# A spectral tower's head stage with the order of a slot changed: a half layer crosses into the next slot

## The chip, the cores and the metric

The kernel runs on one core of one Trainium2 chip. The metric is the device time of one execution in microseconds (us); lower is better. It is written with a queue of instructions for each engine, and the engines wait for each other only by semaphores: TensorE (matrix products and transposes into PSUM banks), ScalarE (activations), VectorE, GpSimd (POOL) and SyncE (SP, which issues the DMAs).

## The reference, cut to what matters

128 images of 64 x 64 with 3 channels go through a tower: a lift to 32 channels with a layer norm, four layers of a spectral convolution plus a pointwise one, and then a head per pixel. The attention and the mixture of experts that follow are not touched by this change.

```
h = layer_norm(x @ fc0_w + fc0_b)
for i in range(4):
    x1 = irfft2(mix of the 2 x 12 x 12 lowest modes of rfft2(h))
    x2 = conv_w[i] h + conv_b[i]
    h = layer_norm(x1 + x2); if i < 3: h = gelu(h)
h = gelu(h @ fc1_w + fc1_b)        # 32 -> 128
h = gelu(h @ fc2_w + fc2_b)        # 128 -> 64
h = h @ fc3_w + fc3_b              # 64 -> 1, one value a pixel
h = h + attention(layer_norm(h)); h = h + ffn(layer_norm(h))
```

## The kernel before

The 128 images are 32 quads of four. Each quad passes the phases stem, layer, layer, layer, head, so that the quads are counted n = 0 to 159, and the quads of the phase "head" are n = 128 to 159. In that phase the fourth layer's output (inverse transform and convolution, then the norm) is made, and the finished pixels of the quad before go through `fc1`, `fc2`, `fc3`. A quad is four slots, k = 0 to 3, and a slot works on one pair of images in two units of half the width, called v and v+1 in the head and `unit`, `unit + 1` in the layer. The head's slots of this kind ("inner") are those of quads 129 to 159, 124 slots, and four closing slots without layer work.

In a slot TensorE runs, in an order written out by hand:

- `inv_h` (L886): the inverse along h into both halves of `ps_y`; `conv` (L893): the convolution, added to one half of `ps_y`, so that ScalarE can read it (`square` L1100, `keep_y` L1104).
- `turn_out` (L905): four transposes of a normalised unit (`normed` L1230 on VectorE) into `ps_t1`; VectorE copies them to `xt` (`take_xt` L1279). These are shown in the trace as `w_raw`, whose room `xt` uses.
- `fc1` (L976 and L983): the first layer for one unit, two products into `ps_f` and two into `ps_s`, each with 32 rows of the array; ScalarE's `g1` (L1123) makes one gelu out of each.
- `fc2` (L992): the second layer for half of a unit, always into the one bank `ps_t2`; ScalarE's `g2` (L1128) empties it. An `fc2` waits for the `g1` of its half and for the `g2` of the half before.
- `fc3` (L1001): the third layer for the whole pair, into `ps_t1`, a slot late; VectorE adds the bias (`take_tok` L1290).
- in slots k = 0 and 2 `inv_w` (L872): the inverse along w of half a quad into `ps_s`, which VectorE transposes (`turn_z` L1211, the name of the memory it writes is `z_second` or `big`). So half of the slots have the inverse and half do not.
- in quads 129 to 135, at the start of slots k = 1 and 3, `mix` (L962): the mixing of modes of the last quads' chunks into `ps_f`, read by VectorE (L1271, L1273) before the next `fc1` may write there.

VectorE also reduces the squares (`sums` L1237) and, each second slot, makes the reciprocal roots of the norm in nine small operations (`rsqrt_half`, L1243 to L1259). Quads 136 to 158 run in a loop of the queues, the others are written out.

Of the kernel before, what the change touches and what calls it, by code (L numbers as in the profile page):

```python
# [7 lines left out]
QUADS = B // 4  # L8
# [18 lines left out]
def vit_tower(nc, x, p, cst, out, scratch):  # L27
# [5 lines left out]
    with ctx:  # L33
# [792 lines left out]
        def _(pe):  # L826
# [35 lines left out]

            def inv_w(n, j, fw_count, g1_count):

                i = n - QUADS
                wait(pe, "y_loaded", 64 * i + 64)
                wait(pe, "iw_read", 2 * i + j)
                wait(pe, "fw_read", fw_count)
                wait(pe, "g1_done", g1_count)
                for sx in range(2):  # L870
                    r = slice(64 * sx, 64 * sx + 64)
                    last = mm(ps_s[:, sx, 0:RUN], c_inw[r, :, :, :].rearrange("p i h w -> p (i h w)"), y_kt[r, j, :],  # L872
                              start=True, stop=True)
                last.then_inc(s["iw_done"], 1)
# [131 lines left out]
            def body(n, q, front, back1, back2, nxt, ph, part=None, chunk=None, seq=None, mixed=0):  # L1006
# [3 lines left out]
                for k in range(4):  # L1010
# [15 lines left out]
                    seen = mixed if part is None or k % 2 == 0 else mixed + (2 if k == 1 else PARTS[part][1] - 2)  # L1026
                    if front is None:
                        iw_count = 2 * LAST
                    else:
                        iw_count = 2 * i + (1 if k == 0 else 3 if k == 3 and nxt in MIXED else 2)  # L1030
                    turned = 2 * (4 * n + k - 3)
                    kind = front if k == 3 else back1
                    fw_head[0] = LAST if back2 not in STORED else (LAST - 1 if k < 1 else LAST)
                    if inner and k == 1 and back2 in STORED:
                        fwd_w(n - 2, 2 * i + 2, 4 * pair)
                    if inner:
                        fc1(2 * pair, 0, iw_count, seen)
                        if not (isinstance(pair, int) and pair == 0):
                            fc3(pair - 1, 2 * pair + 2)
                    if back1 in STORED:  # L1040
                        turn_back(turned - 2, k, 0)
                    if kind is not None and not inner:
                        turn_out(turned, kind, 0, 0)
# [4 lines left out]
                    elif front is not None:  # L1048
# [3 lines left out]
                        conv(k, 0)  # L1052
                    if inner:
                        fc2(2 * pair, 0)
                        if kind is not None:
                            turn_out(turned, kind, 0, pair)
                        fc2(2 * pair, 1)
                        fc1(2 * pair + 1, 1, iw_count, seen)
                    if back1 in STORED:
                        turn_back(turned - 1, k, 1)  # L1060
                    if kind is not None and not inner:
                        turn_out(turned + 1, kind, 1, 0)
                    if front in MIXED:
                        conv(k, 1)
                    if k == 0 and front in MIXED:
                        inv_w(n, 1, LAST if back2 == "head" else n - 2, 4 * pair + 4 if inner else 0)
                    if k == 1 and back2 in STORED and not inner:
                        fwd_w(n - 2, 2 * i + 2 if front in MIXED else 0, 0)
                    if k == 2 and nxt in MIXED:
                        inv_w(n + 1, 0, LAST if back2 == "head" else n - 1, 4 * pair + 4 if inner else 0)  # L1070
                    if inner:
                        fc2(2 * pair + 1, 0)
                        if kind is not None:
                            turn_out(turned + 1, kind, 1, pair)
                        fc2(2 * pair + 1, 1)

            turn_x(0)
            quads(pe, body)
            fc3(4 * QUADS - 1, 8 * QUADS)
            attention_tensor(pe)  # L1080
# [3 lines left out]
        def _(act):  # L1084
# [45 lines left out]
            def body(n, q, front, back1, back2, nxt, ph, part=None, chunk=None, seq=None, mixed=0):  # L1130
# [8 lines left out]
                for k in range(4):  # L1139
# [8 lines left out]
                    if back1 == "head":  # L1148
                        pair = 4 * (n - 1 - LAST) + k
                        for wh in range(2):  # L1150
                            v = 2 * pair + wh
                            if wh == 0 and isinstance(pair, int) and pair == 0:
                                for j in range(2):
                                    act.wait_ge(h_stored[j], 16 * LAST)
                                act.wait_ge(s["t2_done"], 8 * LAST)
                            g1(v, 0)
                            g1(v, 1)
                            if front is not None:
                                square(unit + wh, wh)
                            g2(v, pair, wh, 0)  # L1160
                            if front is not None:
                                keep_y(unit + wh, k, wh)
                            g2(v, pair, wh, 1)
                        continue
# [8 lines left out]

            take_x(0)
            quads(act, body)
            attention_scalar(act)


        @block.vector
        def _(dve):  # L1180
# [25 lines left out]

            def turn_z(n, j):
# [3 lines left out]
                v_.transpose(z_kx[j].rearrange("p (w o) -> p o w", o=32), flat(ps_s).rearrange("p (k o) -> p o k", o=32)  # L1211
                             ).then_inc(s["iw_read"], 1)
# [80 lines left out]
            def body(n, q, front, back1, back2, nxt, ph, part=None, chunk=None, seq=None, mixed=0):  # L1293
                for k in range(4):
# [4 lines left out]
                    if part is not None and k % 2 == 1:  # L1299
                        mix(part, seq, k - 1, 2 if k == 1 else PARTS[part][1] - 2)  # L1300
                    if inner and k == 1 and back2 in STORED:
                        turn_modes(n - 2)
                    if inner:
                        pair = 4 * (n - 1 - LAST) + k
                        if not (isinstance(pair, int) and pair == 0):
                            take_tok(pair - 1, (k - 1) % 4, n - 1 if k else n - 2)
                    if k == 0 and back2 in STORED:
                        turn_w(n - 2, 1)
                    if k == 2 and back2 in STORED and not inner:
# [3 lines left out]
                    if not inner:  # L1313
                        if k == 1 and front in MIXED:
                            turn_z(n, 1)
                        if k == 3 and nxt in MIXED:
                            turn_z(n + 1, 0)
                    for wh in range(2):
                        if kind == "head":
                            take_xt(turned + wh, wh)  # L1320
                        if fresh is not None:
                            normed(2 * (4 * m + kn) + wh, 2 * m + kn // 2, kn, wh)
                        if wh == 0 and k == 3 and front == "stem" and nxt == "stem":
                            copy_x(n + 1)
                        if inner:
                            if front is not None:
                                sums(unit + wh, k, wh)
                            if wh == 0 and k == 0 and front in MIXED:
                                turn_z(n, 1)
                            if wh == 0 and k == 2 and nxt in MIXED:  # L1330
                                turn_z(n + 1, 0)
                    if not inner and front is not None:
                        sums(unit, k, 0)
                        sums(unit + 1, k, 1)
                    if k % 2 and front is not None:
                        rsqrt_half(n, k // 2)

            def newton(eng, step, at, r, t, v):
# [88 lines left out]
```

## Time and profile before

| | |
|---|---|
| median of three runs | 6016.0 us (6007.66 to 6017.28) |
| the profiled execution's own time | 6002.62 us |
| its span | 6000.9 us |
| TensorE busy, share of the span | 5344.9 us, 89% |
| VectorE | 4223.0 us, 70% |
| ScalarE | 3716.5 us, 62% |
| GpSimd | 1170.4 us, 20% |
| `fc2`'s products (L992), of which idle before them | 552.6 us, 93.3 us |

The head stage lies between 3490 and 5250 us from the span's start. Times are those of the hardware profiler in one execution. TensorE's products overlap in its pipeline and their ends are modelled, so what a group takes is best read from its start to the start of the next. "Idle before" names what ended a wait; "issue" means that the profile shows nothing waited for.

### The profile page before, as it was taken

To read this page: it belongs to the slowest core of one execution; us is meant where nothing else is said; L and a number is where in the kernel's file an instruction comes from. 1 tells how busy PE (TensorE), PEld (TensorE's weight loads), DVE (VectorE), ACT (ScalarE), POOL (GpSimd) and SP (SyncE) were. 2 spreads that over 40 slices of the span, in tenths; PEclk is the share of its full clock that TensorE was granted. 3 is DMA by queue.
4 is the path that set the end of the run, shared out by engine and by line. 5 is a ranking of instruction groups with operands and counts; after the bars stand their busy time and mean duration, and the time that the engine had idled before them with its cause. 6 is when DMAs were issued, how large, how long until landed. Compare 5 with 4: busy or idle time off the path is not lost.

```text
span 6000.9 us, 134579 instructions
## 1 busy us (share of the span) xinstructions
PE 5344.9 (89%) x43556; PEld 3023.7 (50%) x43556; DVE 4223.0 (70%) x7712; ACT 3716.5 (62%) x6005; POOL 1170.4 (20%) x1291
## 2 busy tenths in 40 slices
PE   5777789999999999999999988899999999868788
PEld 3444456666666666666666643333333333334443
DVE  5888789999889998999998954444444444444544
ACT  5777676676666676666676655566666666623333
POOL 0266200466000575000664000000000000000000
PEclk9988899999999999999999999999999999967898
DMA  1333567666777666776667733121111111000000
GB/s 64 119 122 128 135 190 217 207 211 215 209 214 213 212 211 206 223 225 212 216 212 211 223 98 74 49 59 43 47 43 50 42 48 46 22 4 7 7 5 6
DMA packets 427386, 756.21 MB, mean 126 GB/s; under 512 B 277809, under 2 KB 335922, under 8 KB 361530
## 3 DMA queue, kind: packets, MB, share of 16 engines
q1 hardware_dynamic: 410682, 714.26, 38.6%
q0 software_dynamic: 16384, 37.78, 2.1%
q8 instruction: 188, 3.08, 0.2%
q14 instruction: 132, 1.08, 0.1%
HBM read 397.49 MB, written 354.42 MB: 125 GB/s over the span
## 4 chain that ended last, share of the span: by engine, by line
PE 77%; DVE 9%; issue 7%; ACT 4%; SPq 1%; POOL 1%; DMA 1%; DVEq 0%; ACTq 0%; POOLq 0%
PE ps_y L893 14%; PE ps_t L905 9%; PE ps_t L992 9%; PE ps_y L886 8%; PE ps_t L914 7%; PE ps_f L976 4%; PE ps_f L927 4%; PE ps_s L872 3%; PE ps_s L940 3%; PE ps_f L962 3%; ACT big L1123 3%; PE ps_t L1001 2%; PE ps_t L328 2%; PE ps_y L861 2%; PE ps_f L318 1%
## 5 line engine op out<-in xcount | busy, mean ns | idle before, releaser
L893 PEld LDWEIGHTS ps_y<-conv_now,big 128*128 128x128 f32 x8192 | 993.4, 192 | 511.5 <-issue 511.5
L1100 ACT ACTIVATE big<-ps_y 128x512 f32<-128x512 f32 x1280 | 773.9, 605 | 702.9 <-PE ps_y L893 631.8
L893 PE MATMUL ps_y<-conv_now,big 128*128 128x128 f32 x8192 | 1147.7, 283 | 0.0
L1230 DVE TENSOR_TENSOR big<-big 128x512 f32<-128x512 f32 x1280 | 876.7, 704 | 114.2 <-PE ps_t L905 108.3
L1237 DVE TENSOR_REDUCE big<-big 128x16 f32<-128x512 f32 x1280 | 843.0, 677 | 103.3 <-ACT big L1100 103.0
L1109 ACT ACTIVATE big<-ps_t 128x512 f32<-128x512 f32 x1024 | 617.2, 603 | 479.4 <-PE ps_t L914 473.6
L905 PE MATMUL ps_t<-ident,big 128*128 128x128 f32 x5120 | 804.9, 281 | 80.2 <-DVE big L1230 78.3
L1116 ACT ACTIVATE big<-ps_t,g_now 128x512 f32<-128x512 f32 x1024 | 801.4, 783 | 56.7 <-PE ps_t L905 55.0
L1104 ACT ACTIVATE big<-ps_y 128x512 f32<-128x512 f32 x1280 | 776.1, 606 | 0.0
L905 PEld LDWEIGHTS ps_t<-ident,big 128*128 128x128 f32 x5120 | 596.7, 143 | 309.5 <-issue 208.4
L914 PE MATMUL ps_t<-ident,big 128*128 128x128 f32 x4096 | 665.0, 286 | 41.5 <-ACT big L1109 41.5
L914 PEld LDWEIGHTS ps_t<-ident,big 128*128 128x128 f32 x4096 | 459.5, 144 | 426.9 <-issue 294.1
L992 PE MATMUL ps_t<-big,fc_w 128*64 128x512 f32 x2048 | 552.6, 614 | 93.3 <-issue 76.9
L1279 DVE COPY w_raw<-ps_t 128x512 f32<-128x512 f32 x256 | 175.6, 686 | 565.1 <-PE ps_t L905 565.1
L1128 ACT ACTIVATE big<-ps_t,fc_b 128x512 f32<-128x512 f32 x512 | 352.4, 688 | 335.7 <-PE ps_t L992 335.7
L1217 DVE STREAM_TRANSPOSE big<-ps_f 128x1024 f32<-128x1024 f32 x256 | 507.8, 1984 | 22.4 <-issue 22.0
L812 POOL COPY x_out<-fw_sb 128x312 f32<-128x312 f32 x256 | 106.9, 445 | 2023.3 <-DVE fw_sb L1223 2023.3
L927 PE MATMUL ps_f<-big,c_fwh 64*32 64x512 f32 x4096 | 362.5, 602 | 54.2 <-issue 40.6
L1123 ACT ACTIVATE big<-ps_f,fc_b 128x1024 f32<-128x1024 f32 x256 | 285.1, 1114 | 159.0 <-PE ps_s L983 106.1
L1211 DVE STREAM_TRANSPOSE z_second<-ps_s 128x1024 f32<-128x1024 f32 x128 | 253.8, 1983 | 117.0 <-PE ps_s L872 117.0
L1211 DVE STREAM_TRANSPOSE big<-ps_s 128x1024 f32<-128x1024 f32 x128 | 250.5, 1957 | 110.8 <-PE ps_s L872 110.8
L797 POOL TENSOR_SCALAR wslot<-w_raw,c_sign 128x576 f32<-128x576 f32 x128 | 327.3, 2557 | 0.0
(175 smaller groups left out, 6842.8 us busy)
## 6 DMA issues: line engine op xcount, KB each, us to landing
hstore<-big SPq DMA_DIRECT2D x256, 1024.0 KB, 4.5
big<-hstore SPq DMA_DIRECT2D x256, 1024.0 KB, 5.2
xmodes<-x_out SPq DMA_DIRECT2D x128, 312.0 KB, 5.0
y_kt<-ymodes SPq DMA_DIRECT2D x512, 78.0 KB
ymodes<-y_st SPq DMA_DIRECT2D x192, 144.0 KB, 3.0
mix_room<-xmodes SPq DMA_DIRECT2D x64, 336.0 KB, 7.4
mix_room<-xmodes SPq DMA_DIRECT2D x64, 288.0 KB, 6.2
ymodes<-y_st SPq DMA_DIRECT2D x64, 192.0 KB, 3.3
```

Source lines behind the costliest of these rows:

```text
L893: last = mm(ps_y[:, wh, 128 * b:128 * b + 128], h_in[k // 2][:, at:at + 128], conv_now[:, :], start=False, stop=(b == 3))
L905: last = nc.tensor.transpose(ps_t1[:, 128 * b:128 * b + 128], xhat[wh][:, 128 * b:128 * b + 128], ident[:, :])
L914: last = nc.tensor.transpose(ps_t2[:, 128 * b:128 * b + 128], h_new[k // 2][:, at:at + 128], ident[:, :])
L927: last = mm(ps_f[at:at + 32, odd, :], c_fwh[r, :], h_px[2 * odd + wh][r, :], start=True, stop=True)
L992: last = mm(ps_t2[64 * i:64 * i + 64, :], fc2_w[:, :], gelu1[2 * pr + i], start=True, stop=True)
L1100: af(y_sq[wh], ps_y[:, wh, :], ACT.Square).then_inc(s["sq_done"], 1)
L1104: af(y_sb[2 * k + wh], ps_y[:, wh, :], ACT.Copy).then_inc(s["y_read"], 1)
L1109: af(h_px[2 * (k % 2) + wh], ps_t2[:, :], ACT.Copy).then_inc(s["px_done"], 1)
L1116: af(h_new[k // 2][:, at:at + 512], ps_t1[:, :], ACT.Identity if kind == "stem" else ACT.Gelu, bias=g_now[:, 1:2], scale=g_now[:, 0:1]).th ...
L1217: v_.transpose(t_w[:, j, :].rearrange("p (k c) -> p c k", c=32), flat(ps_f).rearrange("p (w c) -> p c w", c=32)).then_inc(s["tw_done"], 1)
L1230: v_.tensor_tensor(groups(xhat[wh]), groups(y_sb[2 * k + wh]), rstd[:, k // 2, at:at + 16].unsqueeze(2).to_broadcast([128, 16, 32]), ALU.m ...
L1237: v_.tensor_reduce(ss[:, k // 2, at:at + 16], groups(y_sq[wh]), AX.X, ALU.add).then_inc(s["ss_done"], 1)
```

## The change

Per inner slot the same instructions are issued in another order, on three engines.

- TensorE before: `fc1(v,0)`, `fc3`, `inv_h`, `conv(0)`, `fc2(v,0)`, `turn_out(first)`, `fc2(v,1)`, `fc1(v+1)`, `conv(1)`, [`inv_w`], `fc2(v+1,0)`, `turn_out(second)`, `fc2(v+1,1)`.
- TensorE after: `fc1(v,0)`, `fc2(v-1,1)`, `turn_out(second, of the slot before)`, [`inv_w`], `inv_h`, `fc3`, `conv(0)`, `fc2(v,0)`, `fc1(v+1)`, `turn_out(first)`, `fc2(v,1)`, `conv(1)`, `fc2(v+1,0)`.
- `inv_w` writes `ps_f` in these slots, after the `g1` that read it, and not `ps_s`. `fc1` waits for the reader of the inverse ahead of its `ps_f` half.
- ScalarE and VectorE follow: the last `g2` of a pair, and `take_xt` and `normed` of the second unit, stand at the head of the next slot; `rsqrt_half` stands after `take_tok` of an even slot.
- Outside the inner slots the order is as before.

```diff
-            def inv_w(n, j, fw_count, g1_count):
+            def inv_w(n, j, fw_count, to):
...
-                wait(pe, "g1_done", g1_count)
                 for sx in range(2):
                     r = slice(64 * sx, 64 * sx + 64)
-                    last = mm(ps_s[:, sx, 0:RUN], c_inw[r, :, :, :].rearrange("p i h w -> p (i h w)"), y_kt[r, j, :],
+                    last = mm(to[:, sx, 0:RUN], c_inw[r, :, :, :].rearrange("p i h w -> p (i h w)"), y_kt[r, j, :],
...
                 wait(pe, "tw_done", 2 * LAST)
+                wait(pe, "iw_read", iw_count)
                 wait(pe, "mix_read", mixed)
...
                 wait(pe, "g1_done", 2 * v)
-                wait(pe, "iw_read", iw_count)
...
+            def head_slot(n, k, pair, turned, front, back2, kind, nxt, seen):
...
+                if k == 1 and back2 in STORED:
+                    fwd_w(n - 2, 2 * i + 2, 4 * pair)
+                fc1(v, 0, iw_count, seen)
+                if not opening:
+                    fc2(v - 1, 1)
+                    turn_out(turned - 1, "head", 1, pair - 1)
+                if (k == 0 and front in MIXED) or (k == 2 and nxt in MIXED):
+                    pe.wait_ge(s["g1_done"], 2 * v + 1)
+                    if k == 0:
+                        inv_w(n, 1, 0, ps_f)
+                    else:
+                        inv_w(n + 1, 0, 0, ps_f)
+                if front is not None:
+                    inv_h(n, k)
+                if not opening:
+                    fc3(pair - 1, 2 * pair + 2)
+                if front is not None:
+                    conv(k, 0)
+                fc2(v, 0)
+                fc1(v + 1, 1, iw_later, seen)
+                if kind is not None:
+                    turn_out(turned, kind, 0, pair)
+                fc2(v, 1)
+                if front is not None:
+                    conv(k, 1)
+                fc2(v + 1, 0)
...
+                        g1(v, 0)
+                        if not opening:
+                            g2(v - 1, pair - 1, 1, 1)
+                        g1(v, 1)
+                        if front is not None:
+                            square(unit, 0)
+                            keep_y(unit, k, 0)
+                        g2(v, pair, 0, 0)
+                        g1(v + 1, 0)
+                        g2(v, pair, 0, 1)
+                        g1(v + 1, 1)
+                        g2(v + 1, pair, 1, 0)
+                        if front is not None:
+                            square(unit + 1, 1)
+                            keep_y(unit + 1, k, 1)
...
+                if not opening:
+                    take_xt(turned - 1, 1)
+                    if fresh is not None or k == 2:
+                        late = 2 * (4 * n + k - 3)
+                        normed(late + 1, 2 * n - 2 + (k + 1) // 2, (k + 1) % 4, 1)
+                if k == 0 and front in MIXED:
+                    turn_z(n, 1, ps_f)
+                if k == 2 and nxt in MIXED:
+                    turn_z(n + 1, 0, ps_f)
+                if not opening:
+                    take_tok(pair - 1, (k - 1) % 4, n - 1 if k else n - 2)
+                    if k == 0:
+                        rsqrt_half(n - 1, 1)
+                    if k == 2 and front is not None:
+                        rsqrt_half(n, 0)
+                if front is not None:
+                    sums(unit, k, 0)
+                if kind is not None:
+                    take_xt(turned, 0)
+                if fresh is not None:
+                    normed(2 * (4 * m + kn), 2 * m + kn // 2, kn, 0)
+                if front is not None:
+                    sums(unit + 1, k, 1)
```

## Rows read from the trace of the kernel before

**Rows 1.** Windows view: busy us and counts per engine, then granted clock, DMA.
```profile
4507.21:4534.19 26.98, 24.41 (x150) 9.53 (x148) 12.79 (x25) 17.98 (x24) 0.00 (x0) 1.00 0.17 53
```

**Rows 2.** Timeline (start, duration, engine, operation, [idle before]), a slot without inverse, TensorE.
```profile
4521.56 0.70 PE L976 MATMUL ps_f<-w_raw,fc_w 32*128 32x512 f32 x2
...
4522.63 1.07 PE L1001 MATMUL ps_t<-big,fc_w 128*32 128x512 f32 x8
...
4523.62 1.09 PE L886 MATMUL ps_y<-big,c_inh 32*64 32x512 f32 x8
...
4524.64 1.16 PE L893 MATMUL ps_y<-conv_now,big 128*128 128x128 f32 x8
...
4525.73 1.08 PE L992 MATMUL ps_t<-big,fc_w 128*64 128x512 f32 x4
...
4526.74 0.66 PE L905 MATMUL ps_t<-ident,big 128*128 128x128 f32 x4
...
4527.64 1.08 PE L992 MATMUL ps_t<-big,fc_w 128*64 128x512 f32 x4 [0.25 <-issue]
...
4529.72 1.16 PE L893 MATMUL ps_y<-conv_now,big 128*128 128x128 f32 x8
...
4531.07 1.08 PE L992 MATMUL ps_t<-big,fc_w 128*64 128x512 f32 x4 [0.19 <-ACT big L1123]
...
4532.08 0.66 PE L905 MATMUL ps_t<-ident,big 128*128 128x128 f32 x4
...
4533.19 1.08 PE L992 MATMUL ps_t<-big,fc_w 128*64 128x512 f32 x4 [0.45 <-issue]
...
4534.20 0.70 PE L976 MATMUL ps_f<-w_raw,fc_w 32*128 32x512 f32 x2
```

**Rows 3.** Timeline of the same slot, ScalarE and VectorE.
```profile
4522.81 1.11 ACT L1123 ACTIVATE big<-ps_f,fc_b 128x1024 f32<-128x1024 f32 x1 [0.46 <-PE ps_s L983]
...
4526.85 0.69 ACT L1128 ACTIVATE big<-ps_t,fc_b 128x512 f32<-128x512 f32 x1 [0.34 <-PE ps_t L992]
4527.44 0.59 ACT L1104 ACTIVATE big<-ps_y 128x512 f32<-128x512 f32 x1
4527.54 0.69 DVE L1279 COPY w_raw<-ps_t 128x512 f32<-128x512 f32 x1 [2.86 <-PE ps_t L905]
...
4529.90 1.11 ACT L1123 ACTIVATE big<-ps_f,fc_b 128x1024 f32<-128x1024 f32 x1 [0.46 <-PE ps_s L983]
...
4531.91 0.60 ACT L1100 ACTIVATE big<-ps_y 128x512 f32<-128x512 f32 x1
...
4532.39 0.70 ACT L1128 ACTIVATE big<-ps_t,fc_b 128x512 f32<-128x512 f32 x1
```

**Rows 4.** Timeline of a slot with the inverse along w.
```profile
4517.73 0.97 PE L872 MATMUL ps_s<-y_kt,c_inw 64*128 64x416 f32 x4 [1.19 <-ACT big L1123]
...
4518.63 1.08 PE L992 MATMUL ps_t<-big,fc_w 128*64 128x512 f32 x4
4518.86 1.97 DVE L1211 STREAM_TRANSPOSE z_second<-ps_s 128x1024 f32<-128x1024 f32 x1 [3.77 <-PE ps_s L872]
```

**Rows 5.** Timeline of TensorE in the layer stage.
```profile
2000.27 0.66 PE L905 MATMUL ps_t<-ident,big 128*128 128x128 f32 x4 [0.28 <-DVE big L1230]
2000.86 1.09 PE L886 MATMUL ps_y<-z_second,c_inh 32*64 32x512 f32 x8
```

**Rows 6.** Timelines of TensorE and VectorE where a mixing slot begins.
```profile
3807.11 1.55 PE L962 MATMUL ps_f<-wslot,mix_room 128*32 128x128 f32 x48
...
3808.07 0.56 DVE L1271 TENSOR_REDUCE big<-ps_f 128x12 f32<-128x384 f32 x1
...
3810.42 0.70 PE L976 MATMUL ps_f<-w_raw,fc_w 32*128 32x512 f32 x2 [1.76 <-DVE y_st L1273]
```

**Rows 7.** Timeline of TensorE, an `fc1` whose halves run apart.
```profile
3509.81 1.13 PE L976 MATMUL ps_f<-w_raw,fc_w 32*128 32x512 f32 x4 [0.23 <-DVE y_st L1273]
...
3510.84 1.13 PE L983 MATMUL ps_s<-w_raw,fc_w 32*128 32x512 f32 x4
```

More of the change, by code:

```diff
@@ L1026, in body @@
                     seen = mixed if part is None or k % 2 == 0 else mixed + (2 if k == 1 else PARTS[part][1] - 2)
[L1027 to L1030, printed above, removed]
                     turned = 2 * (4 * n + k - 3)
                     kind = front if k == 3 else back1
[L1033 to L1035 removed]
                     if inner:
[L1037 to L1039 removed]
+                        head_slot(n, k, pair, turned, front, back2, kind, nxt, seen)
+                        continue
                     if back1 in STORED:
                         turn_back(turned - 2, k, 0)
[L1042 removed]
+                    if kind is not None:
                         turn_out(turned, kind, 0, 0)
@@ L1065, in body @@
                     if k == 0 and front in MIXED:
-                        inv_w(n, 1, LAST if back2 == "head" else n - 2, 4 * pair + 4 if inner else 0)
-                    if k == 1 and back2 in STORED and not inner:
+                        inv_w(n, 1, n - 2, ps_s)
+                    if k == 1 and back2 in STORED:
                         fwd_w(n - 2, 2 * i + 2 if front in MIXED else 0, 0)
                     if k == 2 and nxt in MIXED:
-                        inv_w(n + 1, 0, LAST if back2 == "head" else n - 1, 4 * pair + 4 if inner else 0)
@@ L1071, in body @@
[L1071 to L1075, printed above, removed]
+                        inv_w(n + 1, 0, n - 1, ps_s)
+            def head_slot(n, k, pair, turned, front, back2, kind, nxt, seen):
+                i, v, opening = n - QUADS, 2 * pair, isinstance(pair, int) and pair == 0
+                if front is None:
+                    iw_count = 2 * LAST
+                else:
+                    iw_count = 2 * i + (1 if k == 0 else 3 if k == 3 and nxt in MIXED else 2)
+                iw_later = iw_count + (1 if (k == 0 and front in MIXED) or (k == 2 and nxt in MIXED) else 0)
+                fw_head[0] = LAST if back2 not in STORED else (LAST - 1 if k < 1 else LAST)
+                if k == 1 and back2 in STORED:
+                    fwd_w(n - 2, 2 * i + 2, 4 * pair)
[7 more added lines that the diff above has]
+                        inv_w(n, 1, 0, ps_f)
+                    else:
+                        inv_w(n + 1, 0, 0, ps_f)
[7 more added lines that the diff above has]
+                fc1(v + 1, 1, iw_later, seen)
+                if kind is not None:
+                    turn_out(turned, kind, 0, pair)
[3 more added lines that the diff above has]
+                fc2(v + 1, 0)
@@ L1077, in _ @@
             turn_x(0)
             quads(pe, body)
+            fc2(8 * QUADS - 1, 1)
             fc3(4 * QUADS - 1, 8 * QUADS)
@@ L1149, in body @@
                         pair = 4 * (n - 1 - LAST) + k
[L1150 to L1163, printed above, removed]
+                        v, opening = 2 * pair, isinstance(pair, int) and pair == 0
+                        if opening:
+                            for j in range(2):
+                                act.wait_ge(h_stored[j], 16 * LAST)
+                            act.wait_ge(s["t2_done"], 8 * LAST)
+                        g1(v, 0)
[13 more added lines that the diff above has]
+                            keep_y(unit + 1, k, 1)
                         continue
@@ L1210, in turn_z @@
                 dve.wait_ge(s["y_done"], 8 * (n - 1) + 4 * j + 4)
-                v_.transpose(z_kx[j].rearrange("p (w o) -> p o w", o=32), flat(ps_s).rearrange("p (k o) -> p o k", o=32)
+                v_.transpose(z_kx[j].rearrange("p (w o) -> p o w", o=32), flat(of).rearrange("p (k o) -> p o k", o=32)
                              ).then_inc(s["iw_read"], 1)
@@ L1300, in body @@
                         mix(part, seq, k - 1, 2 if k == 1 else PARTS[part][1] - 2)
-                    if inner and k == 1 and back2 in STORED:
-                        turn_modes(n - 2)
                     if inner:
-                        pair = 4 * (n - 1 - LAST) + k
-                        if not (isinstance(pair, int) and pair == 0):
-                            take_tok(pair - 1, (k - 1) % 4, n - 1 if k else n - 2)
+                        head_slot(n, k, unit, turned, front, back2, kind, nxt, fresh, m, kn)
+                        continue
                     if k == 0 and back2 in STORED:
                         turn_w(n - 2, 1)
-                    if k == 2 and back2 in STORED and not inner:
+                    if k == 2 and back2 in STORED:
                         turn_modes(n - 2)
@@ L1312, in body @@
                         turn_w(n - 1, 0)
[L1313 to L1317, printed above, removed]
+                    if k == 1 and front in MIXED:
+                        turn_z(n, 1, ps_s)
+                    if k == 3 and nxt in MIXED:
+                        turn_z(n + 1, 0, ps_s)
                     for wh in range(2):
@@ L1336, in body, with head_slot @@
                         rsqrt_half(n, k // 2)
+            def head_slot(n, k, unit, turned, front, back2, kind, nxt, fresh, m, kn):
+                pair = 4 * (n - 1 - LAST) + k
+                opening = isinstance(pair, int) and pair == 0
+                if k == 0 and back2 in STORED:
+                    turn_w(n - 2, 1)
+                if k == 1 and back2 in STORED:
+                    turn_modes(n - 2)
+                if not opening:
[15 more added lines that the diff above has]
+                    sums(unit, k, 0)
+                if kind is not None:
+                    take_xt(turned, 0)
+                if fresh is not None:
+                    normed(2 * (4 * m + kn), 2 * m + kn // 2, kn, 0)
+                if front is not None:
+                    sums(unit + 1, k, 1)
             def newton(eng, step, at, r, t, v):
```

18 lines of the change are left out of this document (2 added, 16 removed).

## The prediction

> **What bounds the kernel now.** I read the busy table first: TensorE is busy for most of the span and no other engine is close, so the next question is where TensorE still waits. The change touches only the head stage, quads 129 to 159 and the closing one, so I took one window there that holds two slots and nothing else: 26.98 us, TensorE busy for 24.41 of them, ScalarE for 17.98, VectorE for 12.79, at the full granted clock (level 2.4 GHz) [rows 1]. TensorE sets the pace of this stage, and 2.6 us in two slots are waits. Nothing that other engines get back is worth time, except where TensorE waits for it.
>
> The order in time of a slot without inverse comes next [rows 2]. From one `fc1` to the same `fc1` of the next slot it runs 4521.56 to 4534.20, 12.64 us. The reader is to see three places where a group starts late. The second `fc2` of each unit waits behind `turn_out` (idle 0.25 and 0.45), and the first `fc2` of the second unit waits 0.19 for a gelu. The first two are labelled "issue", but [rows 3] name the real releaser: the gelu of `g2` that starts at 4526.85 and lasts 0.69 ends at 4527.54, and `fc2` starts at 4527.64. It is the same at 4532.39 + 0.70 and 4533.19. Both uses of `ps_t2` are one bank, so `fc2` of the second half cannot write until `g2` has emptied it, and only one short group lies between.
>
> In the slot with the inverse along w, `inv_w` idles 1.19 us for the gelu that reads `ps_s` [rows 4]. The two-slot window less the plain slot makes this slot 26.98 − 12.64 = 14.34 us.
>
> **What the waits are really worth.** TensorE's ends are modelled, so I count start to start. In [rows 2]: `fc1` 1.07 (to 4522.63), `fc3` 0.99, `inv_h` 1.02, `conv` 1.09, `fc2` 1.01. For `turn_out` the head shows only stalled cases (0.90 and 1.11); the layer stage shows 0.59 with the next group following at once [rows 5]. The bound above is its recorded 0.66. I take 0.59, since that is the same instruction form. The twelve groups of a plain slot are then two `fc1` 2.14, four `fc2` 4.04, two `turn_out` 1.18, two `conv` 2.18, `inv_h` 1.02, `fc3` 0.99: 11.55 us. So 12.64 − 11.55 = 1.09 us per plain slot is waiting. `inv_w` itself costs 0.90 (4517.73 to 4518.63), so its slot could be 12.45, and 1.89 is waiting there.
>
> **The change part by part.** No instruction is added or dropped in a slot; SP's and POOL's queues keep their order. So the question is only whether each wait, in its new place, is over when TensorE arrives. I lay out a slot from time 0 at `fc1(v,0)`. TensorE, unstalled: `fc2(v-1,1)` 1.07, `turn_out` 2.08, `inv_h` 2.67, `fc3` 3.69, `conv` 4.68, `fc2(v,0)` 5.77, `fc1(v+1)` 6.78, `turn_out` 7.85, `fc2(v,1)` 8.44, `conv` 9.45, `fc2(v+1,0)` 10.54, next slot 11.55.
>
> ScalarE's pieces from [rows 2, 3]: a gelu `g1` can start 1.25 after its `fc1` (4521.56 to 4522.81), lasts 1.11 and lets the next start after 1.00 (two in 2.01, 4529.90 to 4531.91); `g2` can start 1.12 after its `fc2`, lasts 0.69, next after 0.59; a square occupies 0.48, and I take 0.49 for the copy; a release reaches TensorE about 0.06 after the end (4529.90 + 1.11, then 4531.07). Steady state:
> - `g2(v+1,0)` of the slot before starts at 0.11, ends 0.80. Behind it in the queue square 0.70, copy 1.19, so `g1(v,0)` starts at 1.68 instead of 1.25. Nobody needs it before 5.77 in a plain slot.
> - `fc2(v-1,1)` at 1.07 needs that `g2`: 0.86. Margin 0.21.
> - `g2(v-1,1)` 2.68 to 3.37; `fc3` at 3.69 needs it: 3.43. Margin 0.26.
> - `g1(v,1)` done 4.4, needed 6.78.
> - Square and copy of the first half about 5.9 to 6.9, `g2(v,0)` 6.92 to 7.61, needed 8.44; `g1(v+1,0)` 8.03 to 9.14, needed 10.54.
> - `g2(v,1)` 9.56 to 10.25, `fc2(v+1,0)` needs 10.31 and comes at 10.54. Margin 0.23.
> - `g1(v+1,1)` 10.15 to 11.26, released 11.32; the next `fc1`, whose `ps_s` half needs it, comes at 11.55. Margin 0.23.
>
> VectorE: `take_xt` starts 0.80 after a `turn_out` and lasts 0.69 [rows 2, 3], so from 2.08 it is done at 3.57; `fc3` at 3.69 needs it. That margin, 0.06 after the release, is the thinnest. The reciprocal root that moved behind `take_tok` is not needed until a `turn_out` a slot later. Ending the slot with `sums`, VectorE is free again by about 2.1 (square done 1.3, one 0.7 us reduction), before 2.88.
>
> All margins are positive, so a plain slot is 11.55: **1.09 us less.** A missed margin costs only the miss, 0.2 us or so.
>
> **The inverse.** `inv_w` now needs `g1(v,0)`, done at 1.68 + 1.11 + 0.05 = 2.84, and TensorE is there at 2.67: a wait of about 0.2 stays, and behind it everything on TensorE. Its reader, the 1.97 us transpose, starts 1.13 after it [rows 4], so ends near 6.0; the banks `ps_f` are next written by `fc1(v+1)` at 7.9. Covered by four groups (1.02, 0.99, 1.09, 1.01); without them the transpose would cost about 2 us here. Slot: 11.55 + 0.90 + 0.20 = 12.65, **1.69 us less** than 14.34. The modes it reads were loaded two slots earlier, as before.
>
> **The quads that also mix.** In quads 129 to 135 each second slot begins with `mix`, whose `fc1` waits for VectorE [rows 6]. VectorE started on it 0.96 after `mix` began (3807.11 to 3808.07). Now its queue has the second unit's `sums` ahead, and that square ends only at 1.30, so VectorE is free at about 2.0: 1.04 us later, handed on to `fc1` in full. Such a slot gains 1.09 − 1.04 = 0.05. I find no reason for less than nothing except this delay; its bounds are 0.4 (a busy VectorE behind a shorter queue) and 1.7 (one more 0.7 us operation ahead of it).
>
> **Sum.** 24 quads without mixing: 48 × 1.09 + 48 × 1.69 = 133.4. Seven with: 14 × 0.05 + 14 × 1.69 = 24.4. The closing four slots, without layer work, I put at 1 (0 to 4). The `fc2` that now stands behind the loop: nothing, since the old loop ended in the same group. Total 159 us. The profiled execution took 6002.62 (span 6000.9 and 1.7 around it), so 5844; the median of the runs shown is 13.4 above it, so 5857 on their scale. I give 5850, between the two.
>
> **Bounds.** Above: the `inv_w` wait vanishing too gives 62 × 0.2 = 12 more. Below: `turn_out` at 0.66 takes 2 × 0.07 × 124 = 17. Neighbours on TensorE that no row shows (`fc1` before `fc2`, `inv_h` before `fc3`, `fc3` before `conv`, `fc1` before `turn_out`, `inv_w` before `inv_h`) could each cost the same 0.07: 5 × 0.07 × 124 = 43. Two missed margins of 0.2 in each slot: 50. These reach from 5838 to about 5950.
>
> A bubble that repeats on the engine that should be saturated can mean that there is not enough room for the next tile, says the Trainium skill (Perfetto Trace Analysis, Optimization Strategy). Read that way, `ps_t2` is still one bank, an order of instructions gives no room, and the sum would be 0 instead of 159. The rows of this case show that the length of the gap hangs on what stands between two uses of the bank: one `turn_out` leaves 0.25.
>
> **Rivals.**
> - *Everything as laid out* (0.66): 5825 to 5885.
> - *Most of it, with small residues* (0.19): two of the margins of 0.2 are missed by as much in each slot, or the new neighbours cost 0.07 each. 159 − 50 − 43 = 66 at the worst, about 5890 to 5945. For it: four margins of about 0.2 and one of 0.06 in a slot of 11.55, all built of latencies from one place. Against: a miss costs only itself.
> - *One `fc1` split* (0.03): `g1(v+1,1)` comes too late, so the `ps_s` half of the next `fc1` no longer runs beside the `ps_f` half. [Rows 7] show it once: the second half starts 1.03 after the first. 124 × 1.03 = 128, leaving 31: about 5980.
> - *The slower side: both `fc1` split in every slot* (0.07): 2 × 1.03 × 124 = 255, less 159: 96 slower, near 6110. It decides once the splits cost more than 1.3 us a slot (159 / 124). Against it: the second `fc1` has 2.3 us of slack.
> - *The bank still rations* (0.05): the gap moves with `fc2`, `g2` lands as late as before in the shared queue of ScalarE (squares and copies ahead of it), and nothing changes: 6005 to 6028. For it: five of ScalarE's pieces now run back to back from 0.11 to 3.4.
>
> Under 0.2% (12 us) this kernel's measurement can hardly be told from no change. Faster 0.88, same 0.05, slower 0.07. The range takes the first case and most of the second: 5822 to 5935.
>
> **What would show it.** After: two neighbouring slots of about 24.2 us; no idle before `fc2`; `inv_w` to `ps_f` waiting about 0.2 for `g1`; `fc1` with its four parts side by side; ahead of `fc1` in mixing slots a longer wait for VectorE (near 2.8). Wrong if `fc3` waits for `take_xt`, if `fc1`'s `ps_s` half starts a microsecond after its `ps_f` half, or if the plain slot stays above 12.3.

## The result, and the profile after

The change made the kernel faster: 5869.3 us median (5868.2 to 5874.4, four runs) against 6013.2 (6007.7 to 6017.3), ratio 0.976 with a 95% interval of 0.975 to 0.977, or 144 us less. The forecast was 5850 with a range of 5822 to 5935. The profiled execution took 5870.3 us.

Three lines of the page: the span, the engines' busy time and shares, and the group of `fc2`.

```profile
span 5868.6 us, 134909 instructions
...
PE 5338.6 (91%) x43556; PEld 3021.4 (51%) x43556; DVE 4244.8 (72%) x7712; ACT 3689.6 (63%) x6005; POOL 1169.3 (20%) x1291
...
L991 PE MATMUL ps_t<-big,fc_w 128*64 128x512 f32 x2048 | 558.6, 624 | 4.2 <-issue 3.3
```

TensorE does the same work (43556 products) in a shorter span. The page's group of `fc2` had 93.3 us of idle time ahead of it before and has 4.2 now.

One window over two slots of the looped quads answers to [rows 1]: 24.35 us in place of 26.98, and TensorE busy for all but 0.3 of them.

```profile
4502.25:4526.60 24.35, 24.06 (x151) 9.42 (x149) 13.10 (x24) 17.45 (x24) 0.00 (x0) 1.00 0.14 44
```

The timeline of those two slots, TensorE with the ScalarE and VectorE rows that matter, answers to [rows 2 to 4]. Columns are start, duration, engine and line; L976 is `fc1`, L885 `inv_h`, L1303 `take_xt`, L1000 `fc3`, L991 `fc2`, L1140 the gelu `g1`, L871 `inv_w`.

```profile
4502.25 0.70 PE L976 MATMUL ps_f<-w_raw,fc_w 32*128 32x512 f32 x2
...
4504.92 1.09 PE L885 MATMUL ps_y<-big,c_inh 32*64 32x512 f32 x8
4505.14 0.69 DVE L1303 COPY w_raw<-ps_t 128x512 f32<-128x512 f32 x1 [0.87 <-PE ps_t L904]
...
4505.94 1.06 PE L1000 MATMUL ps_t<-big,fc_w 128*32 128x512 f32 x8
...
4510.69 1.08 PE L991 MATMUL ps_t<-big,fc_w 128*64 128x512 f32 x4
...
4512.79 1.08 PE L991 MATMUL ps_t<-big,fc_w 128*64 128x512 f32 x4
...
4513.80 0.70 PE L976 MATMUL ps_f<-w_raw,fc_w 32*128 32x512 f32 x2
...
4514.87 1.08 PE L991 MATMUL ps_t<-big,fc_w 128*64 128x512 f32 x4
...
4515.45 1.13 ACT L1140 ACTIVATE big<-ps_f,fc_b 128x1024 f32<-128x1024 f32 x1
...
4516.82 0.97 PE L871 MATMUL ps_f<-y_kt,c_inw 64*128 64x416 f32 x4 [0.29 <-ACT big L1140]
...
4526.60 0.70 PE L976 MATMUL ps_f<-w_raw,fc_w 32*128 32x512 f32 x2
```

From `fc1` to `fc1` the slot without inverse takes 4513.80 − 4502.25 = 11.55 us, as laid out, with no wait in it. The idle times of 0.25 and 0.45 before `fc2` are gone (the page's 4.2 us are what is left over all of its 2048 products). `take_xt` ends at 4505.83 and `fc3` starts at 4505.94, so the thinnest margin held. The slot with the inverse takes 4526.60 − 4513.80 = 12.80, 0.15 above the forecast: the gelu ends at 4516.58 and `inv_w` starts at 4516.82, 0.24 later. The kernel has 61 slots with the inverse and not 62, since the last quad has no next one: 14 in the mixing quads and 47 behind them, 46 of these in the loop.

The second difference is in the mixing quads, TensorE and then VectorE, answering to [rows 6] (L961 is `mix`, L1261 the reduction `sums`, L1295 the first read of the mixing):

```profile
3566.56 1.55 PE L961 MATMUL ps_f<-wslot,mix_room 128*32 128x128 f32 x48
3570.83 0.70 PE L976 MATMUL ps_f<-w_raw,fc_w 32*128 32x512 f32 x2 [2.72 <-DVE y_st L1297]
...
3572.22 1.98 PE L991 MATMUL ps_t<-big,fc_w 128*64 128x512 f32 x4
...
3596.66 0.89 PE L961 MATMUL ps_f<-wslot,mix_room 128*32 128x128 f32 x24
...
3599.88 0.70 PE L976 MATMUL ps_f<-w_raw,fc_w 32*128 32x512 f32 x2 [2.32 <-DVE y_st L1297]
```

```profile
3567.89 0.69 DVE L1261 TENSOR_REDUCE big<-big 128x16 f32<-128x512 f32 x1 [3.04 <-ACT big L1117]
3568.49 0.55 DVE L1295 TENSOR_REDUCE big<-ps_f 128x12 f32<-128x384 f32 x1
```

The wait before `fc1` grew from 1.76 to 2.72 us. That holds behind the long `mix` of 48 products; behind the short one of 24 it grew from 1.36 to 2.32, so the mixing slots wait by turns for the two lengths. VectorE was kept by `sums` until 3568.49, 1.93 after `mix` began, where it had started 0.96 after. That much was forecast. What follows was not: the `fc2` behind that `fc1` lasts 1.98 where it lasts 1.08 elsewhere. Windows over this slot, over one without the effect, and over the slow products alone (the number after the last "(x0)" is the granted clock):

```profile
3570.83:3584.05 13.22, 13.22 (x72) 5.07 (x72) 4.02 (x6) 7.32 (x9) 0.00 (x0) 0.87 0.00 1
3599.93:3611.58 11.65, 11.65 (x76) 4.66 (x76) 4.01 (x6) 7.32 (x9) 0.00 (x0) 1.00 1.07 169
3572.20:3575.18 2.98, 2.98 (x11) 1.02 (x9) 0.00 (x0) 1.93 (x3) 0.00 (x0) 0.50 0.00 0
```

The granted clock is 0.50 in that stretch: TensorE runs at its lower level, 1.2 of 2.4 GHz. The slot takes 13.22 us in place of 11.65. Of the 14 slots without inverse of the mixing quads, eight have such a stretch in the profiled execution: all six behind a wait of 2.72 us and two of the six behind 2.32, none behind the single one of 2.19 or the opening one of 1.19. They take 13.2 to 14.6 us and lose 14.1 us together. The kernel before had one low stretch there, which cost 1.6.

### The profile page after: what moved, and what is told of

Same layout as the page of the kernel before. It is cut to its first block, busy times and chain, and to the rows that moved or that the text cites. A ratio compares the mean times of both kernels' runs of the same rounds, so it can differ in the third digit from the quotient of the medians.

```text
span 5868.6 us, 134909 instructions
## 1 busy us (share of the span) xinstructions
PE 5338.6 (91%) x43556; PEld 3021.4 (51%) x43556; DVE 4244.8 (72%) x7712; ACT 3689.6 (63%) x6005; POOL 1169.3 (20%) x1291
## 3 DMA queue, kind: packets, MB, share of 16 engines
q14 instruction: 132, 1.08, 0.1%
## 4 chain that ended last, share of the span: by engine, by line
PE 77%; DVE 10%; issue 6%; ACT 4%; SPq 1%; POOL 1%; DMA 1%; DVEq 0%; ACTq 0%; POOLq 0%
PE ps_y L892 17%; PE ps_t L904 9%; PE ps_y L885 9%; PE ps_t L991 8%; PE ps_t L913 7%; PE ps_f L926 4%; PE ps_f L976 4%; PE ps_s L939 2%; PE ps_f L961 2%; PE ps_s L871 2%; PE ps_t L1000 2%; PE ps_t L328 2%; PE ps_y L861 2%; DVE big L1254 1%; PE ps_f L318 1%
## 5 line engine op out<-in xcount | busy, mean ns | idle before, releaser
L1261 DVE TENSOR_REDUCE big<-big 128x16 f32<-128x512 f32 x1280 | 845.4, 678 | 531.6 <-ACT big L1117 531.3
L1121 ACT ACTIVATE big<-ps_y 128x512 f32<-128x512 f32 x1280 | 776.1, 606 | 0.0
L991 PE MATMUL ps_t<-big,fc_w 128*64 128x512 f32 x2048 | 558.6, 624 | 4.2 <-issue 3.3
L1303 DVE COPY w_raw<-ps_t 128x512 f32<-128x512 f32 x256 | 177.0, 692 | 271.2 <-PE ps_t L904 271.2
L1140 ACT ACTIVATE big<-ps_f,fc_b 128x1024 f32<-128x1024 f32 x256 | 286.8, 1120 | 107.1 <-PE ps_s L982 59.7
L976 PE MATMUL ps_f<-w_raw,fc_w 32*128 32x512 f32 x1024 | 292.0, 646 | 38.7 <-DVE y_st L1297 33.6
L982 PE MATMUL ps_s<-w_raw,fc_w 32*128 32x512 f32 x1024 | 292.6, 647 | 0.0
```

Source lines behind the costliest of these rows:

```text
L991: last = mm(ps_t2[64 * i:64 * i + 64, :], fc2_w[:, :], gelu1[2 * pr + i], start=True, stop=True)
L1121: af(y_sb[2 * k + wh], ps_y[:, wh, :], ACT.Copy).then_inc(s["y_read"], 1)
L1261: v_.tensor_reduce(ss[:, k // 2, at:at + 16], groups(y_sq[wh]), AX.X, ALU.add).then_inc(s["ss_done"], 1)
```

## The experiments

Eight runs edit one thing each and one puts four of these edits together. Differences are to the changed kernel's 5869.3 us, in run 4 to the kernel before. Each ratio is to the kernel before, with its interval. The median of the kernel before was 6008.8 to 6013.2 in the sessions of these runs, so a difference between two sessions is sure to about 4 us; where it matters, the slots of the traces decide.

**1. VectorE's last reduction behind the mixing.**

```diff
                     if part is not None and k % 2 == 1:
                         mix(part, seq, k - 1, 2 if k == 1 else PARTS[part][1] - 2)
+                        if inner:
+                            sums(unit - 1, k - 1, 1)
...
-                if front is not None:
+                if front is not None and not later:
                     sums(unit + 1, k, 1)
```

`later` is true in the even slots of the mixing quads, whose last reduction then runs in the odd slot behind.

> In the seven mixing quads VectorE's last reduction of the slot moves behind the mixing work; the rest is the changed kernel. Theory one: VectorE came to the mixing a microsecond late because that reduction, which waits for ScalarE's last square, stood ahead of it in the queue; and the longer idle time of TensorE (2.72 us in place of 1.76) was followed by half the granted clock in 8 of 14 such slots, about 1.6 us each. Then the wait before fc1 goes back to about 1.76, the low-clock stretches nearly vanish, and 14 x 0.96 + 8 x 1.6 = 26 us come back: about 5843 us. Theory two: the wait comes from TensorE's own later start of the mixing, not from VectorE's queue: wait stays near 2.7, about 5869 us.

Measured 5845.7 us, ratio 0.972 (0.969 to 0.975): 24 us less, against 26 expected. The timeline of a mixing slot, all engines:

```profile
3577.36 1.55 PE L961 MATMUL ps_f<-wslot,mix_room 128*32 128x128 f32 x48
...
3578.32 0.56 DVE L1295 TENSOR_REDUCE big<-ps_f 128x12 f32<-128x384 f32 x1 [2.67 <-PE ps_f L961]
...
3580.44 0.68 DVE L1261 TENSOR_REDUCE big<-big 128x16 f32<-128x512 f32 x1
...
3580.68 0.70 PE L976 MATMUL ps_f<-w_raw,fc_w 32*128 32x512 f32 x2 [1.76 <-DVE y_st L1297]
```

VectorE starts 0.96 after `mix` again, and the wait is 1.76 to the hundredth, as before the change. Every later slot without inverse of the mixing quads takes 11.65, and no low stretch is left there but the one at the opening of the stage. Theory one stands: what held VectorE was its own queue, not a late start of the mixing. TensorE's order is that of the changed kernel, so for TensorE only the wait is different, and with it the low stretches are gone.

**2. Work for TensorE inside the wait.**

```diff
-                fc1(v, 0, iw_count, seen)
+                if not mixing:
+                    fc1(v, 0, iw_count, seen)
                 if not opening:
                     fc2(v - 1, 1)
                     turn_out(turned - 1, "head", 1, pair - 1)
+                if mixing:
+                    fc1(v, 0, iw_count, seen)
```

ScalarE's `g1(v, 0)` and `g2(v - 1, ...)` are swapped in these slots too.

> In the mixing slots TensorE runs fc2 of the unit before and the second turn_out between the mixing and fc1 (ScalarE's two gelus are swapped to match); VectorE's queue is that of the changed kernel. Theory one (idle time of TensorE brings the low clock): 1.6 us of work per slot lie in the wait, 14 x 1.6 = 22 us, and with an idle stretch near 1.1 us the 8 low-clock stretches vanish too, 13 us more: about 5834 us. Theory two (the low clock came from the denser work of the new order, not from the wait): the dips stay, about 5847 us. Theory three (VectorE reads mixing results later still because take_xt's data come early): not faster than 5860 us.

Measured 5837.1 us, ratio 0.971 (0.969 to 0.974): 32 us less, 35 expected.

```profile
3564.38 1.08 PE L991 MATMUL ps_t<-big,fc_w 128*64 128x512 f32 x4
...
3565.39 0.66 PE L904 MATMUL ps_t<-ident,big 128*128 128x128 f32 x4
...
3567.17 0.70 PE L976 MATMUL ps_f<-w_raw,fc_w 32*128 32x512 f32 x2 [1.13 <-DVE y_st L1304]
```

`fc1` stands behind a wait of 1.13 us instead of 2.72 (0.64 instead of 2.32 behind the short `mix`), with VectorE as late as in the changed kernel. The low stretches are gone here too, although TensorE's work is as dense as the new order makes it. Against the second theory, then, as in run 1: what goes before the low clock in these slots is the idle stretch, not the density of the work around it.

**3. The new order, with the inverse in the second gelu's banks.**

```diff
-                    pe.wait_ge(s["g1_done"], 2 * v + 1)
+                    pe.wait_ge(s["g1_done"], 2 * v + 2)
                     if k == 0:
-                        inv_w(n, 1, 0, ps_f)
+                        inv_w(n, 1, 0, ps_s)
...
```

The inverse of slot k = 2, VectorE's `turn_z` and the wait for it in `fc1` go back to `ps_s` with it.

> The new order is kept, but the inverse along w goes to the second gelu's banks again, as before the change, and so waits for the gelu that reads those. Theory one: the bank matters because the second gelu is released 1.6 us after the first (about 4.45 against 2.84 from the slot's start), and everything on TensorE stands behind: 62 x 1.5 = 93 us, about 5960 us. Theory two: crossing the slot alone carries the gain, the wait is hidden: about 5869 us.

Measured 6024.2 us, ratio 1.002 (1.001 to 1.003): the whole gain is gone, 155 us where 93 were expected. First TensorE around the inverse, then windows over an inverse slot, a slot without, and the stretch behind the wait.

```profile
4508.94 1.54 PE L871 MATMUL ps_s<-y_kt,c_inw 64*128 64x416 f32 x4 [1.87 <-ACT big L1140]
4510.41 1.98 PE L885 MATMUL ps_y<-z_second,c_inh 32*64 32x512 f32 x8
```

```profile
4504.34:4520.30 15.96, 14.09 (x78) 5.00 (x76) 8.41 (x17) 8.71 (x12) 0.00 (x0) 0.89 0.21 68
4520.30:4531.85 11.55, 11.55 (x75) 4.56 (x73) 4.71 (x7) 8.71 (x12) 0.00 (x0) 1.00 0.00 0
4508.94:4512.30 3.36, 3.35 (x12) 0.61 (x12) 1.67 (x1) 0.00 (x0) 0.00 (x0) 0.54 0.00 0
```

The wait of 1.87 is the expected one, 1.6 longer. But the products behind it run at half the clock (0.54 over 3.36 us), and the slot takes 15.96. Of the 46 looped inverse slots, 39 took about 16.0 and 7 took 14.38, which is the 12.80 of the changed kernel and the wait alone. So 61 × 1.6 = 98 us are the wait, and 39 × 1.6 = 62 of the low clock come on top; by slots the head stage is 164 us longer, and the rest lies in the mixing quads. The expectation had left out the same thing as the prediction had.

**4. The order of before, with the inverse in the first gelu's banks.**

```diff
-                        inv_w(n, 1, LAST if back2 == "head" else n - 2, 4 * pair + 4 if inner else 0)
+                        inv_w(n, 1, LAST if back2 == "head" else n - 2, 4 * pair + 3 if inner else 0, ps_f if inner else ps_s)
```

> The kernel before, with only the inverse along w moved to the first gelu's banks (its place in the order is kept). Theory one: it waits for one gelu instead of two, 1.0 us less in 62 slots: 62 us, about 5951 us, and the 0.25 and 0.45 us waits before fc2 stay. Theory two: the wait before the inverse only moves to the fc2 behind it, which needs that second gelu's data late anyway: no more than 10 us, about 6005 us.

Measured 5945.8 us, ratio 0.989 (0.987 to 0.991): 66 us less than before, 62 expected. The looped inverse slots fall from 14.34 to 13.34 and 13.42, the others stay at 12.64. The bank is worth the same one gelu in the old order, and the other 77 us of the change's 144 come with the crossing. The two are not independent: without the bank the crossing leaves the time where it was (run 3). Its plain slot keeps the 11.55 us there, and its inverse slot takes 14.38 without a low stretch, as 14.34 before; so it is the low clock, about 1.6 us in most inverse slots, that eats the gain of the plain ones.

**5. The gelu's wait last.**

```diff
-                    pe.wait_ge(s["g1_done"], 2 * v + 1)
...
                 wait(pe, "fw_read", fw_count)
+                wait(pe, "g1_done", g1_count)
```

> The changed kernel, with the wait of the inverse along w for the first gelu put behind its other waits (loaded modes, earlier reader) instead of ahead of them. Theory one: the inverse started 0.24 us after that gelu's end, not 0.06, because TensorE's sequencer had two more waits on counts held in registers to work through once the gelu was there: in the looped quads the inverse slot falls from 12.80 to about 12.62 (what the last, written out, quad shows), 47 x 0.18 = 8 us, about 5861 us. Theory two: the 0.24 is what a hand-over from ScalarE to this product costs: 12.80 stays, 5869 us.

Measured 5858.7 us, ratio 0.975 (0.973 to 0.976): 11 us less, 8 expected. The times alone can't show it, since this interval overlaps the changed kernel's (0.975 to 0.977); the slots can. In this kernel L1140 is `g1` and L872 `inv_w`:

```profile
4507.47 1.13 ACT L1140 ACTIVATE big<-ps_f,fc_b 128x1024 f32<-128x1024 f32 x1
...
4508.65 0.97 PE L872 MATMUL ps_f<-y_kt,c_inw 64*128 64x416 f32 x4
```

The gelu ends at 4508.60 and the inverse starts 0.05 later, in place of 0.24. The slot takes 12.61 in place of 12.80 in all 46 looped cases, 9 us together. Theory one stands for the loop. In the quads that are written out, where the counts are constants, it is the other way round. First the changed kernel, with the gelu's wait ahead, then this run, with it last:

```profile
3555.61 1.13 ACT L1140 ACTIVATE big<-ps_f,fc_b 128x1024 f32<-128x1024 f32 x1
...
3556.79 0.97 PE L871 MATMUL ps_f<-y_kt,c_inw 64*128 64x416 f32 x4
```

```profile
3555.65 1.13 ACT L1140 ACTIVATE big<-ps_f,fc_b 128x1024 f32<-128x1024 f32 x1
...
3556.92 0.97 PE L872 MATMUL ps_f<-y_kt,c_inw 64*128 64x416 f32 x4 [0.19 <-ACT big L1140]
```

From the gelu's end to the inverse it is 0.05 with the wait ahead and 0.14 with it last, in the 15 written-out cases (to a hundredth). So the late place is cheap in the loop (0.05 against 0.24) and dear outside it (0.14 against 0.05); why was not tried.

**6. The last copy behind the next gelu.**

```diff
                         g1(v, 0)
+                        if not opening and (k == 0 or k == 2 and front is not None):
+                            keep_y(unit - 1, (k - 1) % 4, 1)
...
                             square(unit + 1, 1)
-                            keep_y(unit + 1, k, 1)
+                            if k % 2 == 0:
+                                keep_y(unit + 1, k, 1)
```

> The changed kernel, with ScalarE's last copy of the slot moved behind the first gelu of the next one where the inverse along w follows. Theory one: that gelu starts 0.4 us late because square and copy stand ahead of it; without the copy it starts at 1.25 from the slot's start, ends 2.4, and TensorE, which comes at 2.67, finds it done: the inverse slot falls from 12.80 to 12.45, 62 x 0.35 = 22 us, about 5847 us. Theory two: the copy's delay now holds the inverse along h (it needs both halves of ps_y read): the wait moves there, 5869 us or more.

Measured 5850.5 us, ratio 0.973 (0.971 to 0.975): 19 us less, 22 expected.

```profile
4506.66 1.11 ACT L1140 ACTIVATE big<-ps_f,fc_b 128x1024 f32<-128x1024 f32 x1
...
4507.67 0.59 ACT L1121 ACTIVATE big<-ps_y 128x512 f32<-128x512 f32 x1
...
4508.08 0.97 PE L871 MATMUL ps_f<-y_kt,c_inw 64*128 64x416 f32 x4
```

`g1` starts 0.4 us earlier in its slot, the copy (L1121) follows, and the inverse has no wait left: the slot is 12.44, its 11.55 and the inverse's 0.90.

**7. `fc3` ahead of `inv_h`.**

```diff
+                if not opening:
+                    fc3(pair - 1, 2 * pair + 2)
                 if front is not None:
                     inv_h(n, k)
-                if not opening:
-                    fc3(pair - 1, 2 * pair + 2)
```

> The changed kernel with fc3 ahead of inv_h instead of behind it. Theory one: fc3 then stands right behind the turn_out whose copy out of the same bank it must wait for, about 0.97 us in each slot without inverse; in slots with the inverse inv_w covers it. 62 x 0.97 = 60 us, about 5929 us, with no more low-clock stretches than the changed kernel has. Theory two: waits of a microsecond bring the low clock here too, as the 1.9 us waits did: 1.6 us more in most of those slots, over 6000 us. Theory three: VectorE's copy is not what fc3 would wait for: 5869 us.

Measured 5943.4 us, ratio 0.989 (0.987 to 0.991): 74 us more, 60 expected.

```profile
4508.62 1.06 PE L1000 MATMUL ps_t<-big,fc_w 128*32 128x512 f32 x8 [0.89 <-DVE w_raw L1303]
```

`fc3` now waits 0.89 for VectorE's copy, and the looped slot without inverse takes 12.50 in place of 11.55, 0.96 more; with the inverse it stays 12.80. No low stretch comes with it in the looped quads. 63 slots of 0.96 make 60 of the 74 us. In the mixing quads the 13 slots behind a `mix` now wait ahead of `fc1` and ahead of `fc3`, and all 13 have a low stretch, where 8 had one in the changed kernel. One of them (clock 0.88):

```profile
3614.94:3629.09 14.15, 13.32 (x73) 5.09 (x73) 4.01 (x6) 7.32 (x9) 0.00 (x0) 0.88 0.90 140
```

So theory one is wrong in its last clause: more low stretches did come. By slots the head stage is 68 us longer, 60 from the waits and about 7 from these stretches; the other 6 us of the medians are not in the head stage of this trace. This shows what covers the copy: `inv_h` in its place of 1.02 us, with the thin margin.

**8. The edits of runs 1, 2, 5 and 6 together.**

> The changed kernel with four edits together: VectorE's last reduction behind the mixing, TensorE's fc2 and turn_out between mixing and fc1, the gelu wait of the inverse last, ScalarE's last copy behind the next gelu. If the four are independent: from 5837 us of the filled mixing slots 14 x 0.95 = 13 less for the earlier VectorE and 22 less for the inverse slots, about 5802 us. If the edits share one wait (the filling already hides what the earlier VectorE gives), about 5815 us.

Measured 5807.0 us, ratio 0.966 (0.965 to 0.968): 62 us below the changed kernel and the fastest version here. It lies between the two expectations, nearer the first. The looped slots are 11.54 and 12.44, which is TensorE's work without any wait.

**9. The second unit's turn in its own slot.** The other two parts of the change stay.

```diff
                     fc2(v - 1, 1)
-                    turn_out(turned - 1, "head", 1, pair - 1)
...
                     conv(k, 1)
+                if kind is not None:
+                    turn_out(turned + 1, kind, 1, pair)
                 fc2(v + 1, 0)
```

VectorE's `take_xt` of that unit moves back into the slot with it.

> The changed kernel with the third named part undone: the second unit's turn_out stays in its own slot (between the second convolution and fc2 of the second unit), while fc2's last half still crosses and the inverse along w still goes to the first gelu's banks. Theory one: that turn_out is not what frees fc2 (fc2 and its gelu cross without it), but it covers two later waits: without it fc3 comes at 3.10 from the slot's start and waits 0.3 for the crossed gelu, and the inverse comes at 2.08 and waits 0.9 in place of 0.36. 62 x 0.33 + 62 x 0.58 = 56 us: about 5925 us. Theory two: without it the waits of 0.25 and 0.45 before fc2 return, more than 1 us a slot, near 6000 us. Theory three: it carries nothing: 5869 us.

Measured 5913.2 us, ratio 0.983 (0.981 to 0.986): 44 us more, 56 expected.

```profile
4502.32 0.97 PE L871 MATMUL ps_f<-y_kt,c_inw 64*128 64x416 f32 x4 [0.87 <-ACT big L1141]
...
4511.52 1.08 PE L991 MATMUL ps_t<-big,fc_w 128*64 128x512 f32 x4
...
4513.60 1.08 PE L991 MATMUL ps_t<-big,fc_w 128*64 128x512 f32 x4
...
4516.13 1.06 PE L1000 MATMUL ps_t<-big,fc_w 128*32 128x512 f32 x8 [0.43 <-ACT big L1146]
```

The inverse waits 0.87 in place of 0.29 and `fc3` 0.43 for the crossed gelu (its releaser is ScalarE's L1146), while no `fc2` waits: 11.89 and 13.24 us a slot. These are 0.34 and 0.44 more than in the changed kernel; 0.33 and 0.58 were expected, and the inverse's share is what the expectation had too large. The crossing of `fc2` is what removes the old waits; the turn only fills the time until the crossed gelu and the first one are done.

## Why the prediction was right, point by point

- **Plain slot, 1.09 us less.** Right: 12.64 to 11.55 in the looped quads. No wait exceeds its margin, not even the 0.06 of `take_xt`, and the neighbours on TensorE that no row had shown cost nothing. `turn_out` at 0.59 was the right choice.
- **The inverse's slot, 1.69 less.** The mechanism is right (run 3 and run 4), the size a little off: 1.54. The term "done at 1.68 + 1.11 + 0.05" took 0.05 for the hand-over, and it was 0.24, because in the looped quads the gelu's wait stood ahead of two others (run 5). About 7 us over the 46 looped slots. That ScalarE's copy makes this gelu 0.4 late is shown by run 6; the square ahead of it was not moved in any run.
- **Mixing quads, "Such a slot gains 1.09 − 1.04 = 0.05".** Here is the mis-sized term. The later VectorE was right in place and size (0.97 for 1.04; runs 1 and 2), but the step that handed it on to `fc1` priced the wait at its own length. Eight of the waits were followed by half the clock, 14.1 us, against one before, 1.6. Run 1 gives both back together. The row of 1.76 us was taken for all of these slots, but half of them have the short `mix` and 1.36; the growth of 0.96 is the same in both.
- **Sum.** 159 forecast. By slots, the profiled pair has 24 × 2 × 2.63 = 126 us in the looped part and 139 us from the first `fc1` to the last `fc3` (1759 to 1620 us); the medians differ by 144. The missing 15 to 20 us are the two terms above, 7 and 12.5 (14.1 less the 1.6 that the kernel before lost too).
- **Slips in the working that change little.** The sum counts 62 inverse slots, and there are 61 (0.6 us). The three terms below the forecast, 17, 43 and 50, reach to 5960 and not to about 5950; the plain slot met none of them.
- **The rivals.** No `fc1` ran split. The bank no longer rations: nothing waits for `ps_t2`. The reading of the Trainium skill (Perfetto Trace Analysis, Optimization Strategy), that a repeated bubble can mean missing room, would have kept the gap; the 93.3 us before `fc2` fell to 4.2 with the same single bank. What was enough is one group of about 1.07 us between two uses, an `fc1` or a `conv`, in place of a `turn_out` of 0.59: the changed order has a `conv` alone between two of its `fc2` and an `fc1` alone between two others, with margins of 0.23 and 0.21 in the prediction's layout.

## What to carry to other kernels

A gap that repeats before the user of a single bank can be taken out by the order alone: move the second use behind enough work that does not need the bank, even into the next iteration, and lay the slot out to a hundredth with the releases of every other queue. Then look at what stands last in each other engine's queue, because the next iteration's first consumer waits behind it: here a reduction of 0.7 us cost 24 us (about half of it through the low clock) and a copy of 0.6 us cost 19. Price a wait of TensorE not by its length alone. Where several semaphores are waited for, the place of the latest one is worth a look in the trace: last was better in the loop, ahead was better in the written-out code.

## What the runs showed of the hardware that was not expected

- The lower clock level came after some waits of about 2 us and added about 1.6 us to the price of each. Counted over one profiled execution of each kernel, by the idle time between `mix` and `fc1`: after 1.36 us none of 18 slots had it, after 1.76 one of 21 (the kernel before, runs 1 and 4); after 2.19 or 2.32, 26 of 42, and after 2.72, 28 of 36 (the changed kernel, runs 3, 5, 6, 7 and 9). The opening slot, with 1.19, had it in one of these six. Ahead of `inv_w` in run 3 it came after 1.68 in 2 of 14 slots and after 1.87 in 39 of 46. Length is not all: in run 3 all six waits of 2.32 were followed by it and three of the six of 2.72, in the changed kernel two of six and all six. In the loop of run 3 the slots that escaped are regular, each seventh or eighth inverse slot. What else decides was not tried and stays open. The Trainium skill (TensorE: Matmul & The Clock Gate, "A second HAM failure mode: psum-queue depth-cycling") describes short idle stretches between groups of products as a cause of such swings between the two levels; the rows of run 3 agree, 0.54 of the clock behind an idle stretch of 1.87 us.
- In the loop, where the counts of the waits are held in registers, a wait on TensorE that is satisfied late costs 0.19 us more when two further waits stand behind it (0.24 against 0.05 from the gelu's end to the product, run 5). In the written-out quads, with constants, it costs 0.09 more when it stands last (0.14 against 0.05).
